# A fused retrieval-scoring kernel: most PSUM banks of tiles 1 to 3 seeded with the bias and copied out by ScalarE

## What is computed

```
retrieved = mean(item_embeddings[indices], axis=1)      # indices past the table read its last row
fused     = concatenate([user_rep, retrieved]) @ W_fuse + b_fuse
logits    = fused @ W_proj + b_proj                     # 512 x 12500, float32
```

## Time and profile before

| | us |
|---|---|
| median of 3 runs | 323.04 (322.44 to 324.77) |
| profiled execution | 324.66, its span 322.8 |
| busy in the span: TensorE, VectorE, ScalarE, GpSimd | 298.1, 256.1, 134.9, 73.8 |
| mean granted TensorE clock | 0.984 |

### The profile page before, as it was taken

One profiled execution on the slowest core, in us unless ns is written; L12 is line 12 of the kernel. 1 busy time (PEld: TensorE's weight loads), 2 busy tenths in 40 slices (PEclk: granted clock), 3 DMA queues, 4 the chain that ended last, 5 costly groups with the idle time before them and its releaser, 6 DMA issues. The chain is left out here.

```text
span 322.8 us, 4017 instructions
## 1 busy us (share of the span) xinstructions
PE 298.1 (92%) x1371; PEld 242.7 (75%) x1371; DVE 256.1 (79%) x373; ACT 134.9 (42%) x171; POOL 73.8 (23%) x76
## 2 busy tenths in 40 slices
PE   3999798879989999799299999999999999999995
PEld 1559686768878898587187888888888888888884
DVE  5888989759768569958799897998979799797223
ACT  2205455310010032654456568465655845564220
POOL 5768782777776000000000000000000000000000
PEclk9999999999999999989789999999999999999999
DMA  7999999895995202638458493975849487163315
GB/s 274 351 363 324 372 389 378 250 337 159 367 351 179 97 32 97 225 105 310 185 187 320 162 353 125 305 268 179 329 137 350 151 279 292 65 190 125 127 67 190
DMA packets 32480, 75.43 MB, mean 234 GB/s; under 512 B 4390, under 2 KB 20532, under 8 KB 32461
## 3 DMA queue, kind: packets, MB, share of 16 engines
q1 hardware_dynamic: 25340, 58.31, 51.1%
q0 software_dynamic: 5536, 14.04, 13.0%
q10 hardware_dynamic: 1584, 2.84, 2.3%
HBM read 52.84 MB, written 25.60 MB: 243 GB/s over the span
## 5 line engine op out<-in xcount | busy, mean ns | idle before, releaser
L419 POOL DMA_INDIRECT ring<-item_embeddings,rows x56 | 59.1, 1056 | 19.5 <-issue 14.9
L1172 PE MATMUL pair<-w_hi,s_hi 128*128 128x500 f32 x144 | 56.2, 390 | 0.1
L1174 PE MATMUL pair<-w_lo,s_hi 128*128 128x500 f32 x144 | 56.2, 390 | 0.0
L1175 PE MATMUL pair<-w_hi,s_lo 128*128 128x500 f32 x144 | 56.1, 389 | 0.0
L1172 PE MATMUL pair<-w_hi,f_hi 128*128 128x500 f32 x108 | 43.6, 404 | 8.5 <-ACT f_sum L580 6.2
L1097 PE MATMUL pair<-w_hi,f_hi 128*128 128x500 f32 x112 | 44.3, 395 | 6.3 <-DVE f_lo L818 5.5
L1097 PE MATMUL pair<-w_lo,f_hi 128*128 128x500 f32 x112 | 43.9, 392 | 0.0
L769 DVE SCALAR_TENSOR_TENSOR pair<-ring,mask,pair 128x512 f32<-128x512 f32 x48 | 36.1, 752 | 9.7 <-DMA ring<-item_embeddings,rows 6.7
L1097 PE MATMUL pair<-w_hi,f_lo 128*128 128x500 f32 x112 | 43.7, 390 | 0.0
L1175 PE MATMUL pair<-w_hi,f_lo 128*128 128x500 f32 x108 | 43.1, 399 | 0.0
L1174 PE MATMUL pair<-w_lo,f_hi 128*128 128x500 f32 x108 | 43.1, 399 | 0.0
(11 more groups left out here) (137 smaller groups left out, 422.1 us busy)
## 6 DMA issues: line engine op xcount, KB each, us to landing
w_raw<-w_proj SPq DMA_DIRECT2D x28, 500.0 KB, 7.6
logits<-part_out SPq DMA_DIRECT2D x24, 500.0 KB, 3.3
early<-w_proj SPq DMA_DIRECT2D x22, 500.0 KB, 6.1
logits<-out_sb SPq DMA_DIRECT2D x23, 250.0 KB, 2.4
logits<-out_sb SPq DMA_DIRECT2D x11, 500.0 KB, 3.6
s_sum<-b_proj SPq DMA_DIRECT2D x10, 250.0 KB, 6.6
odd_bias<-b_proj SPq DMA_DIRECT2D x8, 250.0 KB, 6.8
logits<-out_sb ACTq DMA_DIRECT2D x7, 250.0 KB, 6.6
```

The source lines that it names most:

```text
L419: return nc.gpsimd.indirect_dma_start(out=to, out_offset=None, in_=table, in_offset=bass.IndirectOffsetOnAxis(ap=column, axis=0), **how)
L1172: nc.tensor.matmul(ps[:, q, 0:CHUNK], f, hi, start=start and k == 0, stop=False, skip_group_check=True)
L1174: nc.tensor.matmul(ps[:, q, 0:CHUNK], f, lo, start=False, stop=False, skip_group_check=True)
L1175: m = nc.tensor.matmul(ps[:, q, 0:CHUNK], f_rest, hi, start=False, stop=stop and k == 1, skip_group_check=True)
```

## The change

Tiles 0 and 1 get 10 slots, and the positions of home and laps change. `SEEDED` names 14 of the 21 chunks of tiles 1 to 3: for them ScalarE copies the bias into the bank before the first matmul (`seed`), TensorE accumulates onto it, and ScalarE copies the bank out (`evacuate_here`). `wait_bank` names the last user of a bank among chunks and turns. The other seven stay with VectorE: (1,0), (1,1), (1,2), (2,2), (3,2), (3,5) and (3,6). VectorE's list is written out anew: the third sort goes behind f_lo of tile 1, all adds of tiles 2 and 3 behind f_lo of the tile before, and the evacuations of round 0 ahead of more of round 1's splits. SP loads round 1's blocks of column 1 before tile 3's stores, and its bias after (3,1). The bias rows 4 to 6 go to `lists`. Left out of the diff are the new semaphore, and one argument that tells `project` that a bank is seeded.

```diff
@@ -19,21 +19,22 @@
 UNITS = 7
 
 
-SLOTS = (11, 11, 17, 17)
+SLOTS = (10, 10, 17, 17)
 LISTING = 2
 LISTED = 7
 SORTED = 24
 RING = 12
 USES = tuple(n + (t < LISTING) for t, n in enumerate(SLOTS))
 START = tuple(sum(USES[:t]) for t in range(TILES))
-HOME_AT = (2, 4, 2, 2)
-LAPS_AT = (8, 10, 8, 8)
+HOME_AT = (2, 4, 5, 4)
+LAPS_AT = (9, 9, 10, 10)
 DVE_FIRST = 7
 PE_FIRST = SLOTS[0] - DVE_FIRST
 PE_LAST = 0
 AHEAD = 5
 TURN_EVERY = RESIDENT + 1
-HOME_AFTER = (0, 7, 6, 6)
+HOME_AFTER = (0, 7, 10, 10)
+SEEDED = ((), (3, 4, 5, 6), (0, 1, 3, 4, 5, 6), (0, 1, 3, 4))
 FAR = 1024.0
 OUT_SLOTS = 3
 BIAS_SLOTS = 8
@@ -137,6 +138,7 @@
 
         spots = lists[:, 0:LISTING * LISTED, :].rearrange("p (t j) m -> p t j m", t=LISTING)
         later = lists[:, LISTING * LISTED, :]
+        late_bias = lists[:, :, :].rearrange("p j m -> p (j m)")
         places_i = ring[:, RING - 1, 0:P].bitcast(I32)
         token = listing[:, 0, 0, 1:2]
         fused_ps = banks[0:HK]
@@ -235,8 +238,9 @@
             return (w_hi, w_lo)[of][:, 2 * c + k // 2, k % 2, :]
 
         def bias_of(c):
-            slot = (c + HK) % BIAS_SLOTS
-            return bias[:, slot:slot + 1, 0:CHUNK]
+            if c < HK:
+                return bias[:, HK + c:HK + c + 1, 0:CHUNK]
+            return late_bias[:, (c - HK) * 512:(c - HK) * 512 + CHUNK].unsqueeze(1)
 
         def pair_chunk(i, j):
             return RESIDENT + 2 * i + j
@@ -288,11 +292,24 @@
         def group_of(t, c):
             return RESIDENT * t + c
 
+        def by_scalar(t, c):
+
+            return t == 0 or c in SEEDED[t]
+
+        def nth_seeded(t, c):
+            return sum(len(SEEDED[u]) for u in range(t)) + SEEDED[t].index(c)
+
         def wait_evacuated(engine, g):
-            if g < RESIDENT:
-                engine.wait_ge(first_evacuated, g + 1)
-            else:
-                engine.wait_ge(evacuated, g - RESIDENT + 1)
+            t, c = divmod(g, RESIDENT)
+            here = by_scalar(t, c)
+            n = sum(by_scalar(*divmod(x, RESIDENT)) == here for x in range(g))
+            engine.wait_ge(first_evacuated if here else evacuated, n + 1)
+
+        def wait_bank(engine, t, c):
+
+            before_t, before_c = divmod(TURN_EVERY * t + c - 3, TURN_EVERY)
+            if before_t >= 0 and before_c < RESIDENT:
+                wait_evacuated(engine, group_of(before_t, before_c))
 
         block = ctx.enter_context(nc.Block())
 
@@ -336,8 +353,11 @@
             for c in range(2, RESIDENT):
                 load_chunk(c)
             for b in range(RESIDENT):
-                if b % HK == 0:
-                    sp.wait_ge(lo_ready, 2 * HK if b == 0 else 2 * RESIDENT)
+                if b == 0:
+                    sp.wait_ge(lo_ready, 2 * HK)
+                elif b == HK:
+                    sp.wait_ge(packed, LISTING)
+                    sp.wait_ge(lo_ready, 2 * (RESIDENT - 1))
                 load_bias(b)
 
             def load_block(i, k, j):
@@ -371,17 +391,18 @@
                         load_block(0, c // 2 - 1, j)
             for c in range(RESIDENT):
                 store(2, c)
+            for k in range(2):
+                load_block(1, k, 1)
             for c in range(RESIDENT):
                 store(3, c)
+                if c == 1:
+                    sp.wait_ge(f_ready, HK * TILES)
+                    load_pair_bias(1)
                 if c == 3:
+                    sp.wait_ge(s_lo_ready, 2)
+                    load_pair_bias(0)
                     for k in range(2):
                         load_block(1, k, 0)
-                if c == 4:
-                    sp.wait_ge(s_lo_ready, 2)
-                    load_pair_bias(0)
-            for k in range(2):
-                load_block(1, k, 1)
-            load_pair_bias(1)
             for i in range(ROUNDS):
                 if i + 2 < ROUNDS:
                     sp.wait_ge(unit_lo, units_made(i, B22))
@@ -502,16 +523,22 @@
                 nc.scalar.activation(ret_t[:, j, :], ident[:], ACT.Copy,
                                      scale=mask[:, 1, last_add(1) + j + 2:last_add(1) + j + 3]).then_inc(kept_ready, 1)
 
-            def evacuate_first(c):
-                act.wait_ge(projected, c + 1)
-                if c >= OUT_SLOTS:
-                    act.wait_ge(out_stored[c % OUT_SLOTS], 16 * (c // OUT_SLOTS))
-                nc.scalar.copy(out_sb[:, c % OUT_SLOTS, :], group_bank(0, c)[:, 0:CHUNK]).then_inc(first_evacuated, 1)
+            def evacuate_here(t, c):
+                g = group_of(t, c)
+                act.wait_ge(projected, g + 1)
+                if g >= OUT_SLOTS:
+                    act.wait_ge(out_stored[g % OUT_SLOTS], 16 * (g // OUT_SLOTS))
+                nc.scalar.copy(out_sb[:, g % OUT_SLOTS, :], group_bank(t, c)[:, 0:CHUNK]).then_inc(first_evacuated, 1)
 
             def store_first(c):
-                act.wait_ge(first_evacuated, c + 1)
+                wait_evacuated(act, c)
                 act.dma_start(out_dram[0, :, c * CHUNK:(c + 1) * CHUNK], out_sb[:, c % OUT_SLOTS, :])\
                   .then_inc(out_stored[c % OUT_SLOTS], 16)
+
+            def seed(t, c):
+                wait_bank(act, t, c)
+                act.wait_ge(bias_landed[c], 16)
+                nc.scalar.copy(group_bank(t, c)[:, 0:CHUNK], bias_of(c)[:, 0, :]).then_inc(seeded, 1)
 
             act.wait_ge(ident_ready, 1)
             act.wait_ge(mask_ready, 1)
@@ -533,19 +560,41 @@
             split_hi(2, (1,))
             fused_hi(0, (2, 3))
             split_hi(3)
-            for c in range(RESIDENT):
-                if c == RESIDENT - 1:
-                    mean(1)
-                evacuate_first(c)
-                if c < PE_LAST:
-                    keep_last(c)
+            for c in range(RESIDENT - 1):
+                evacuate_here(0, c)
                 store_first(c)
                 if c + 4 < RESIDENT:
                     split_hi(c + 4)
+            mean(1)
             fused_hi(1)
-            for t in range(2, TILES):
-                mean(t)
-                fused_hi(t)
+            evacuate_here(0, RESIDENT - 1)
+            store_first(RESIDENT - 1)
+            seed(1, 3)
+            seed(1, 4)
+            seed(1, 5)
+            evacuate_here(1, 3)
+            seed(1, 6)
+            evacuate_here(1, 4)
+            evacuate_here(1, 5)
+            seed(2, 0)
+            mean(2)
+            fused_hi(2)
+            evacuate_here(1, 6)
+            seed(2, 1)
+            evacuate_here(2, 0)
+            seed(2, 3)
+            evacuate_here(2, 1)
+            seed(2, 4)
+            seed(2, 5)
+            evacuate_here(2, 3)
+            seed(2, 6)
+            evacuate_here(2, 4)
+            evacuate_here(2, 5)
+            seed(3, 0)
+            mean(3)
+            fused_hi(3)
+            evacuate_here(2, 6)
+            seed(3, 1)
 
             def s_hi_of(q):
                 act.wait_ge(s_summed, q + 1)
@@ -597,10 +646,18 @@
                 nc.scalar.copy(c_ps[:, :, 0:CHUNK], pair_bias[i % 2][0].unsqueeze(1).to_broadcast([P, 2, CHUNK]))\
                   .then_inc(c_seeded, 1)
 
+            evacuate_here(3, 0)
+            seed(3, 3)
             s_hi_of(0)
+            evacuate_here(3, 1)
+            seed(3, 4)
             unit_hi_of(0, B11)
             s_hi_of(1)
-            for u in range(T2, UNITS):
+            unit_hi_of(0, T2)
+            evacuate_here(3, 3)
+            unit_hi_of(0, B21)
+            evacuate_here(3, 4)
+            for u in range(T3, UNITS):
                 unit_hi_of(0, u)
             seed_b(0)
             seed_c(0)
@@ -824,8 +881,7 @@
                 dve.wait_ge(projected, g + 1)
                 if g >= OUT_SLOTS:
                     dve.wait_ge(out_stored[g % OUT_SLOTS], 16 * (g // OUT_SLOTS))
-                if t == 1:
-                    dve.wait_ge(bias_landed[c], 16)
+                dve.wait_ge(bias_landed[c], 16)
                 nc.vector.tensor_tensor(out_sb[:, g % OUT_SLOTS, :], group_bank(t, c)[:, 0:CHUNK], bias_of(c)[:, 0, :],
                                         ALU.add).then_inc(evacuated, 1)
 
@@ -950,72 +1006,82 @@
             add(1, 4)
             add(1, 5)
             split_lo(4)
-            sort(3)
-            add(1, 6)
-            add(1, 7)
-            split_lo(5)
+            add_pair(1, 6)
             add_home(1)
             add(1, 8)
+            split_lo(5)
+            add(1, 9)
             split_lo(6)
-            for i in range(9, last_add(1) + 1):
-                add(1, i)
-            for t in range(TILES):
-                for c in range(RESIDENT):
...
-                if t + 2 < TILES:
-                    add(t + 2, 4)
+            fused_lo(1)
+            add_last(2)
+            sort(3)
+            add_pair(2, 0)
+            evacuate(1, 0)
+            add_pair(2, 2)
+            evacuate(1, 1)
+            add_pair(2, 4)
+            add(2, 6)
+            evacuate(1, 2)
+            add_pair(2, 7)
+            add_pair(2, 9)
```

(110 more changed lines are left out.)

## The result

The changed kernel takes 315.4 us, the median of four executions (312.3 to 315.9), against 323.9 for the kernel before beside it; the ratio is 0.9728, with a 95% interval of 0.966 to 0.9795. So it is 2 to 3.4% faster. The forecast was 312.7. The profiled execution was the fastest: 312.27, its span 310.4, at a granted clock of 1.0; the others ran at 0.989 to 0.993.

The account below looks back on a forecast made before the run. VectorE's program order was taken to bound the start of TensorE's unbroken half. 0.1 us up to tile 3 plus 10.2 from there to round 2 made 10.3 off the median 323.0: 312.7 us, range 309.5 to 317.5.

Parts of the forecast that it names:

- The bound: Whole kernel: TensorE sets the end, VectorE's program order sets when TensorE's unbroken half, 145.70 us long, starts.
- Tile 1's f_lo: Before tile 1: the 2.35 us wait behind an add waiting for its gather goes; tile 1 starts at 66.0.
- Tile 2's sum is late: Turn of tile 2: VectorE starts the sum after f_lo(1), needs 19.7 us, and TensorE stalls 2.7 us.
- Chunk 6: Tile 0's last chunk load: lands 0.5 us sooner, bounds 2.0 sooner to 2 later.
- Rival A: Tile 0: chunk 6 lands 2 us later because gathers share the DMA engines; 315.2 us, chance 0.12.
- Tile 3's start: Tile 3 starts at about 116.1 us, against 116.2 before; sign of being right: within 1 us of 116.
- the 10 us chain: VectorE from tile 3's sums to round 2: 10.6 us go, 0.4 is new, balance 10.2 us.
- Rival B: Turn of tile 2: the clock falls at the new 2.7 us stall, costing 1.7 us; 314.4, chance 0.12.
- the main line: Whole kernel: the forecast with no rival happening, 10.3 us off, 312.7 us; chance 0.60.
- The sum without a fall: Profiled execution: 10.3 us off the span, 322.8 to 312.5, and 314.4 with the 1.9 us around it.
- rival C: From tile 3 on: ScalarE becomes the bound, nine late handoffs give back 4.5 to 9 us; 317 to 322, chance 0.13.
- rival D: Tiles 0 and 1: the list of extra rows overflows, falling back to laps, over 400 us more; chance 0.03.

Follow-up runs that it names:

- three parts taken away: Changed kernel, one at a time: without ScalarE's seeds and copies 323.3 us; with SP's old load order 320.4; with VectorE's old round 0 order 317.3.
- The runs that fill the gaps: Changed kernel with work of tile 2's sum moved ahead of tile 1's f_lo, 311.0 us; also tile 3's ahead of tile 2's f_lo, 308.4 and 308.8.
- the best kernel: Changed kernel with first adds of tiles 2 and 3 ahead of the preceding f_lo and evacuation (1,1) behind three more adds: 308.4, again 308.8 us.

## Why the prediction was right, and where it was off

**The bound.** Right: the unbroken half costs the same, and everything is decided by when VectorE lets it start. Each of three parts taken away made VectorE's way to round 2 longer, by 3.1, 5.0 and 2.3 us, together 10.4 of the 47.58 - 37.03 = 10.55 gained there. The prediction had 10.2. They were taken away one at a time, so that they add up so well is not itself shown. Over the whole kernel they don't: 7.9, 5.0 and 1.9 us are 14.8, more than the gain, because the new order in tiles 1 to 3 loses time by itself and ScalarE's part pays for it.

**Tile 1's f_lo.** Right: the wait of 2.3 us is gone.

**Tile 2's sum is late.** Right in mechanism and size: the hole was said to be 2.7 us and is 3.17; that of tile 3 0.7 and is 0.98. VectorE needs 84.60 - 64.55 = 20.05 us from the share to the last add where the sum of rows gave 19.7. The runs that fill the gaps show the cause by taking it away.

**Chunk 6.** The step that was off. It said 0.5 us sooner with a bound of 2.0, "all of SP's lead"; the trace has 2.65. Rival A (later) fell. The bound was taken from the wrong thing: the last two loads of chunk 6 are issued from 36.81 us in place of 37.58, only 0.8 sooner, and over the profiles the issue doesn't go with the cast (37.94 and 50.9 in the second profile of the changed kernel, 36.87 and 56.19 with 11 slots). So what changed is how long the transfers took once issued. The DMA engines were as full as before but moved more, 390 GB/s from 28 to 52 us against 357 in the kernel before, so a share near 1.0 was not the limit it was taken for. What let them move more is not shown. And where the cast falls differs between executions: in the second profile of the same kernel it starts at about 50.9, 1.8 us sooner than in the first. One profile of before was compared with a forecast finer than that. Why the medians move by only some 0.5 us for a slot, when the profiles' casts lie further apart, stays open: the other executions leave no trace. The issue of chunk 6's loads and the DMA columns from 28 to 52 us, each first before, then after:

```profile
37.58 3.40 SPq L305 DMA_DIRECT2D early<-w_proj  x2
...
36.81 3.40 SPq L322 DMA_DIRECT2D early<-w_proj  x2
```
```profile
28.00:52.00 24.00, 21.35 (x125) 18.55 (x124) 21.92 (x51) 12.93 (x21) 17.66 (x14) 1.00 0.99 357
28.00:52.00 24.00, 20.89 (x115) 17.94 (x115) 23.00 (x43) 13.59 (x21) 19.05 (x15) 1.00 1.03 390
```

**Tile 3's start.** 114.3, not 116.1, so the sign "within 1 us of 116" was missed: the 10 us chain then hung on a start 1.8 us sooner, T3 of round 1 came at 162.9 in place of 165, and the profiled execution came out at 312.3, 12.4 off its predecessor, where 10.3 were forecast (314.4).

**The clock.** Rival B is what most executions seem to do: three of four ran at 0.989 to 0.993, and the one profile at 0.989 has the fall. It had a chance of 0.12 and a price of 1.7 us, for one fall; that profile shows it behind the hole at the turn, at 1.3 us, and a second one at tile 0. The forecast took it as an alternative to the main line, while it comes on top of it.

**The number.** 312.7 lies near the profiled 312.3 by luck. The sum without a fall gave 314.4, and chunk 6 made that 2.1 too late. The other executions took 3.1 more than the profiled one, of which the second profile shows some 2.0 with the two falls and 1.1 as a later start. And 1.7 us had been taken off because the kernel before was profiled in an execution 1.7 above its median, while the changed kernel was profiled in its fastest. -2.1 + 3.1 + 1.7 makes the 2.7 by which the median, 315.4, is over the forecast.

**ScalarE (rival C).** It fell. Its 14 seeds and 14 copies made VectorE wait 0.22 us once before s_hi, where 0.4 was put in. No evacuation of VectorE's runs at the same time as a seed, but its adds into a bank do: the pair at 69.58 us, with the seed at 69.69 beside it, takes 1.61 us, and the one at 74.04 in the kernel before, with ScalarE idle, 1.60. The Trainium skill says in PSUM — Partial Sum Buffer, Specifications (TRN2), that the two reach PSUM in parallel at full rate while they keep to different banks; the trace agrees. The extra rows fit their lists (rival D): no further laps in the trace.

## What to carry to other kernels

Follow the engine whose list is in program order, and write down its idle time in front of each wait: a gap of 5.8 us before a wait and a hole of 3.2 us behind the work that follows are one thing, and moving independent work across the waits gave 6.6 us (315.4 to 308.8). A hole costs its length and, if the clock falls behind it, here 1.3 to 1.7 us more, so price both in the main line. Before counting an earlier load as a gain, look whether the next wait in the chain is for the same thing. And before taking a part for carrying the gain, take it away alone: here the new order without the other engine's help began the sums behind tile 3 5.9 us later than the old one.

## What was not expected of the hardware

The clock isn't settled by the length of a hole. Behind the same 2.34 us before tile 0's first chunk it was 1.0 in one profile of the changed kernel and 0.50 for 2.70 us in another; behind 3.17 us it was 1.0 in the one, and 0.59 over 3.5 us behind 2.97 us in the other. What TensorE did before the hole was the same list of instructions. Behind the 0.98 us at tile 3's turn neither of the two shows a fall. Over all profiles of the kernels above: behind a hole of 3.0 to 3.7 us at a turn the clock fell in six of seven cases, behind one of 1.0 to 1.2 us in none of seven, and behind the 1.9 to 2.3 us before tile 0's first chunk in three of twelve.

Not tried: T1's sum of round 0 could fill the 5.6 us that VectorE still waits before f_lo of tile 3 in the best kernel. The sums share their memory with the fuse weights and the turned rows that tile 3 still needs, so they would need a buffer of their own.
